# Turning and placing the rank stacks on VectorE and ScalarE instead of TensorE

## Chip, cores and metric

The kernel runs on one core of one Trainium2 chip. The metric is the device time in microseconds; each kernel is run several times and the median counts. TensorE multiplies 128x128 blocks; VectorE and ScalarE do elementwise work and may read PSUM, POOL (GpSimd) works on SBUF alone here, and the SP queue issues all DMAs.

## The reference, cut to what matters

x has 64 sequences of 64 tokens with 1024 features. Four residual layers are applied in a row, each with its own per-sequence choice:

```
x = x + (x W0^T + 2 * sum over experts of gate * (x A0^T) B0^T)   # top 2 of 8 experts, language bias on the gate
x = x + W1[condition]^T x                                         # 64x64 mixing of the 64 tokens of a sequence
x = x + (x B2[a]^T) A2[a]^T                                       # rank 16, adapter a of 64
x = x + (x W3^T + b3 + 2 * (x A3[m]) B3[m])                       # rank 16, adapter m of 32
```

The kernel multiplies the dense layers together beforehand (W0 and W3 with their identities, and the small matrices of the adapters through them), so that one pass over x is left, plus the products of low rank. For the two adapters it has to form the hidden values h2 and h3 (16 per sequence), and multiply them with rows of the combined adapter matrices.

## The kernel before, in words

**Tiling.** A tile is 128 tokens, that is two sequences of 64 (BT = 2, TB = 64); there are 32 tiles, handled in 16 pairs (a, b). Every fp32 operand of a product is split into a rounded high part and a low rest, and three matmuls (high-high, high-low, low-high) make one product. Half of the work is cut by one level of Winograd's form of Strassen's method, which takes four sums of blocks of x (S1 to S4) per pair. They are made by POOL (sums, L715), rounded by ScalarE (s_hi) and their rests taken by VectorE (s_lo).

**Stages.** Up to about 346 us the weights are combined (groups of matmuls, L1407). After that the pairs run: step(j) for j = 0 to 14 and last(15). Each engine has its own program, written out by hand in order, with semaphores between them: fore(j) (TensorE L1522, ScalarE L964, VectorE L1314), then the rest of step(j) (L1585, L986, L1339) or last(j) (L1622, L1007, L1360). POOL's order is in L739 and L755. In numbers(j), a and b are the tiles of pair j, a1 and b1 those of the pair before, and b2 = 2j-3 is the odd tile of the pair before those two, whose last product is finished at the start of pair j. back is set from the second pair on, fin from the third on (14 pairs).

**The ranks.** For a tile, the mixed products (L1458) leave the hidden values of both adapters in the first 64 columns of an output bank. For h2:
- ScalarE rounds them to the high part (h2_hi, L892), two instructions of 64 partitions, one per sequence, into h2stack, a 128x128 tile with the axes sequence, rank, copy, high or low. A sequence fills only its own 64 columns; the rest was zeroed once by POOL (L645, L646).
- VectorE writes the low part (h2_lo L1219, stack_lo L1212), again two instructions.
- TensorE transposes the stack to PSUM (h2_rows, L1484), ScalarE copies it to SBUF as h2T (h2T_copy, L907).
- TensorE multiplies h2T with the adapter rows up2 (ranks2, L1499), which adds h2's part to the output and yields h3's hidden values (semaphore pe_h3).

h3 goes the same way over h3_hi (L899), h3_lo (L1225), h3_rows (L1489), h3T_copy (L911) and ranks3 (L1509). Then add_bias (L1262) adds the bias to the three pieces of the bank and writes the output tile outb, and only after that (semaphores dve_out) may the next tile's mixed products use the bank.

**Order around the change.** At the start of a pair VectorE does h3_lo(b2), Ra_raw, Lb_lo, Ra_lo of the pair before, add_bias(b2), x1_lo, h2_lo(a1), the hidden sums and the gates. TensorE does the plain product of tile a with the transpose of h3(b2) after three of its eight blocks and ranks3(b2) after five, the hidden product, then mixed(a1), which waits for Ra_lo and all three pieces of add_bias(b2). POOL starts its sums after place_udb(a1) (L708), which waits for the last ranks2 (pe_up2). In the calm middle of the pair come h2(a1), h3(a1) and h2(b1). The last pair has the same parts in an order of its own.

Of the kernel before, what the change touches and what calls it, by code (L numbers as in the profile page):

```python
# [16 lines left out]
def build(nc, x, stat, mov, a0, wr, wc, u3, u2k, d3k, bias3, lang_ids, ids, out):  # L17
# [137 lines left out]
    with ctx:  # L155
# [116 lines left out]
        h2stack = sb("h2stack", [P, BT, RANK, 2, 2], F32R)  # L272
        h3stack = sb("h3stack", [P, BT, RANK, 2, 2], F32R)
# [26 lines left out]
        ps_hgT, ps_h2T, ps_h3T = ps_s[:, 0:TOKENS], ps_s[:, TOKENS:2 * TOKENS], ps_s[:, 2 * TOKENS:3 * TOKENS]  # L300
# [10 lines left out]
        def plain_bank(t):  # L311

            return ps_d[0] if (t // 2 + t) % 2 == 0 else ps_d[2]

# [5 lines left out]
        def sem(name):  # L320
# [21 lines left out]
        act_h2, act_h2T, act_h3, act_h3T, act_hgT = map(sem, ("act_h2", "act_h2T", "act_h3", "act_h3T", "act_hgT"))  # L342
# [7 lines left out]
        dve_h2, dve_h3, dve_hgT = map(sem, ("dve_h2", "dve_h3", "dve_hgT"))  # L350
# [6 lines left out]
        pe_group, pe_hl, pe_ud, pe_rep, pe_h, pe_mix, pe_h2T, pe_h3, pe_up2, pe_hgT, pe_h3T = map(  # L357
            sem, ("pe_group", "pe_hl", "pe_ud", "pe_rep", "pe_h", "pe_mix", "pe_h2T", "pe_h3", "pe_up2", "pe_hgT", "pe_h3T"))
# [3 lines left out]
        CONSTS = 6  # L362
        SETS = BT + 8
# [14 lines left out]
        def _(sp):  # L378
# [189 lines left out]
            sp.wait_ge(pool_const, CONSTS)  # L568
# [68 lines left out]
        def _(pool):  # L637
# [7 lines left out]
            nc.gpsimd.memset(h2stack[:, :, :, :, :].rearrange("p b r h e -> p (b r h e)").bitcast(F32), 0.0).then_inc(pool_const, 1)  # L645
            nc.gpsimd.memset(h3stack[:, :, :, :, :].rearrange("p b r h e -> p (b r h e)").bitcast(F32), 0.0).then_inc(pool_const, 1)  # L646
# [124 lines left out]
        def _(act):  # L771
# [120 lines left out]
            def h2_hi(t):  # L892
                act.wait_ge(pe_h, t + 1)
                for b in range(BT):
                    rows = slice(b * TB, (b + 1) * TB)
                    last = round_to(h2stack[rows, b, :, :, 0], hidden(t, rows, slice(b * RANK, (b + 1) * RANK)))
                last.then_inc(act_h2, 1)

            def h3_hi(t):  # L899
                act.wait_ge(pe_h3, t + 1)  # L900
                for b in range(BT):
                    rows = slice(b * TB, (b + 1) * TB)
                    last = nc.scalar.activation(h3stack[rows, b, :, :, 0], hidden(t, rows, slice(BR + b * RANK, BR + (b + 1) * RANK)),
                                                ACT.Copy, scale=SCALE3)
# [59 lines left out]
            def fore(j, back, fin):  # L964
                a, b, a1, b1, b2 = numbers(j)
                if fin:
                    h3_hi(b2)
                if back:
                    Ra_hi(j - 1)
                if fin:  # L970
                    h3T_copy(b2)
# [3 lines left out]
                if back:  # L975
                    h2_hi(a1)
                gate_exp(a)
                ud_hi(b)
                after_P1(j)
                if back:  # L980
                    h2T_copy(a1)
# [4 lines left out]
            def step(j, back, fin):  # L986
# [10 lines left out]
                if back:  # L997
                    h2_hi(b1)
                ud_hi(a + 2)
# [3 lines left out]
                if back:  # L1003
                    h2T_copy(b1)
# [35 lines left out]
        def _(dve):  # L1040
# [88 lines left out]
            nc.vector.tensor_scalar(rbias[:, :, :], rbias[:, :, :], LANG_BIAS, None, ALU.mult).then_inc(dve_set, 1)  # L1129

# [8 lines left out]
            dve.wait_ge(dve_set, BT + 7)  # L1139
# [72 lines left out]
            def stack_lo(t, rows, b, cols, stacked, scale):  # L1212

                src = out_bank(t, 0)[rows, cols][:, :, None].to_broadcast([TB, RANK, 2])
                return nc.vector.scalar_tensor_tensor(out=stacked[rows, b, :, :, 1], in0=src, scalar=scale,
                                                      in1=stacked[rows, b, :, :, 0].bitcast(F32), op0=ALU.mult,
                                                      op1=ALU.subtract)

            def h2_lo(t):  # L1219
                dve.wait_ge(act_h2, t + 1)  # L1220
                for b in range(BT):
                    last = stack_lo(t, slice(b * TB, (b + 1) * TB), b, slice(b * RANK, (b + 1) * RANK), h2stack, 1.0)
                last.then_inc(dve_h2, 1)

            def h3_lo(t):  # L1225
                dve.wait_ge(act_h3, t + 1)
                for b in range(BT):
                    last = stack_lo(t, slice(b * TB, (b + 1) * TB), b, slice(BR + b * RANK, BR + (b + 1) * RANK), h3stack, SCALE3)
                last.then_inc(dve_h3, 1)

# [167 lines left out]
        def _(pe):  # L1398
# [85 lines left out]
            def h2_rows(t):  # L1484
                pe.wait_ge(dve_h2, t + 1)
                nc.tensor.transpose(ps_h2T, h2stack[:, :, :, :, :].rearrange("p b r h e -> p (b r h e)").bitcast(F32),
                                    ident[:, :]).then_inc(pe_h2T, 1)

            def h3_rows(t):  # L1489
                pe.wait_ge(dve_h3, t + 1)  # L1490
                nc.tensor.transpose(ps_h3T, h3stack[:, :, :, :, :].rearrange("p b r h e -> p (b r h e)").bitcast(F32),
                                    ident[:, :]).then_inc(pe_h3T, 1)

# [5 lines left out]
            def ranks2(t):  # L1499
                pe.wait_ge(act_h2T, t + 1)  # L1500
# [8 lines left out]
            def ranks3(t):  # L1509
                pe.wait_ge(act_h3T, t + 1)  # L1510
# [11 lines left out]
            def fore(j, back, fin):  # L1522
# [9 lines left out]
                plain(a, range(0, 3))  # L1532
                if fin:
                    h3_rows(b2)
# [226 lines left out]
```

## Time and profile before

| | |
|---|---|
| median of 3 runs | 904.51 us (903.81 to 905.5) |
| the profiled execution | 906.27 us |
| span of its profile | 904.5 us |
| TensorE busy, granted clock | 895.8 us (99%), 1.00 |
| VectorE busy | 557.5 us (62%) |
| ScalarE busy | 345.8 us (38%) |
| POOL busy | 234.9 us (26%) |

Times in the profile count from the start of the span, in microseconds. The profiled execution is one run, 1.8 us of which lie outside the span. L12 is line 12 of the kernel above. A row that names one engine's instruction may end with the idle time before it and who ended it.

### The profile page before, as it was taken

The page shows a single profiled execution, that of the slowest core. Times are in us where ns is not written, and L with a number is a line of the kernel's source. Part 1 is how long each engine was busy: PE and PEld are TensorE (multiplying, and loading weights), DVE is VectorE, ACT ScalarE, POOL GpSimd, SP SyncE. Part 2 cuts the span into 40 slices and gives each one's busy share as a digit, 9 for nine tenths or more (in the row PEclk, how much of TensorE's full clock was granted, in tenths as well). Part 3 has the DMA queues.
Part 4 walks back from the last instruction along what each step waited for, and adds up shares of the span by engine and source line. Part 5 has one row for each costly group of instructions (what it writes and reads, how often), then busy time and mean ns, then how long its engine had stood idle before and what let it go on. Part 6 is the DMA issues. An engine that isn't in the chain of part 4 may idle for free.

```text
span 904.5 us, 14862 instructions
## 1 busy us (share of the span) xinstructions
PE 895.8 (99%) x4758; PEld 795.4 (88%) x4758; DVE 557.5 (62%) x1421; ACT 345.8 (38%) x800; POOL 234.9 (26%) x379
## 2 busy tenths in 40 slices
PE   9999999999999999999999999999999999999997
PEld 7888888888888888998998998998998999989997
DVE  6655444354357526567667677677676676676675
ACT  5543343333334333333434433434424334334333
POOL 1000010011010003523424433424415325324240
PEclk9999999999999999999999999999999999999999
DMA  7978686999663564666766766766666567666664
GB/s 248 309 252 287 208 252 202 311 338 270 186 190 119 172 211 132 189 179 185 218 181 189 216 188 182 210 194 192 190 197 213 168 189 226 182 174 216 184 199 155
DMA packets 105602, 187.69 MB, mean 208 GB/s; under 512 B 15926, under 2 KB 66870, under 8 KB 105526
## 3 DMA queue, kind: packets, MB, share of 16 engines
q1 hardware_dynamic: 105526, 186.76, 67.7%
q8 instruction: 38, 0.62, 0.3%
q14 instruction: 38, 0.31, 0.1%
HBM read 143.20 MB, written 49.81 MB: 213 GB/s over the span
## 4 chain that ended last, share of the span: by engine, by line
PE 92%; DMA 3%; SPq 2%; issue 1%; POOL 1%; DVE 0%; ACT 0%; DVEq 0%; POOLq 0%
PE ps_o L1407 28%; PE ps_d L1433 17%; PE ps_w L1441 13%; PE ps_d L1441 10%; PE ps_s L1407 9%; PE ps_o L1454 5%; PE ps_d L1448 4%; PE ps_o L1465 2%; DMA mdraw<-t 2%; PE ps_s L1471 1%; SPq L445 1%; PE ps_w L1448 1%; DMA chunk_a_raw<-mov 1%; SPq L473 1%; PE ps_o L1503 1%
## 5 line engine op out<-in xcount | busy, mean ns | idle before, releaser
L1042 DVE TENSOR_TENSOR stat_lo<-stat_raw,stat_hi 128x1024 fp32r<-128x1024 f32 (+1 forms) x127 | 146.3, 1152 | 25.8 <-ACT stat_hi L773 23.5
L773 ACT ACTIVATE stat_hi<-stat_raw 128x1024 fp32r<-128x1024 f32 (+1 forms) x127 | 116.8, 933 | 20.5 <-POOL stat_raw L657 6.3
L1433 PE MATMUL ps_d<-w_hi,stat_hi 128*128 128x512 f32 x256 | 105.0, 410 | 0.0
L1433 PE MATMUL ps_d<-w_lo,stat_hi 128*128 128x512 f32 x256 | 101.1, 395 | 0.0
L1433 PE MATMUL ps_d<-w_hi,stat_lo 128*128 128x512 f32 x256 | 100.8, 394 | 0.0
L1407 PE MATMUL ps_o<-chunk_a_hi,stat_hi 128*128 128x512 f32 x216 | 84.4, 391 | 0.6 <-DVE chunk_a_lo L1042 0.6
L1407 PE MATMUL ps_o<-chunk_a_lo,stat_hi 128*128 128x512 f32 x216 | 84.1, 389 | 0.0
L1407 PE MATMUL ps_o<-chunk_a_hi,stat_lo 128*128 128x512 f32 x216 | 84.0, 389 | 0.0
L682 POOL CAST w_hi<-mdraw 128x512 fp32r<-128x512 f32 x32 | 19.6, 614 | 208.8 <-DMA mdraw<-t 208.8
L657 POOL TENSOR_TENSOR stat_raw<-stat_raw,ident 128x128 f32<-128x128 f32 x40 | 21.8, 546 | 186.3 <-DMA stat_raw<-stat 186.3
L1407 PE MATMUL ps_o<-chunk_b_hi,stat_hi 128*128 128x512 f32 x152 | 59.1, 389 | 0.0
L1407 PE MATMUL ps_o<-chunk_b_hi,stat_lo 128*128 128x512 f32 x152 | 59.1, 389 | 0.0
L1407 PE MATMUL ps_o<-chunk_b_lo,stat_hi 128*128 128x512 f32 x152 | 59.1, 389 | 0.0
L1433 PEld LDWEIGHTS ps_d<-w_lo,stat_hi 128*128 128x128 f32 x256 | 48.1, 188 | 11.4
L1433 PEld LDWEIGHTS ps_d<-w_hi,stat_hi 128*128 128x128 f32 x256 | 48.5, 189 | 9.8 <-DVE udb L1246 0.3
L1433 PEld LDWEIGHTS ps_d<-w_hi,stat_lo 128*128 128x128 f32 x256 | 48.4, 189 | 8.1
L1259 DVE TENSOR_TENSOR outb<-ps_o,bias_row 128x356 f32<-128x356 f32 (+1 forms) x93 | 42.0, 507 | 13.1 <-PE ps_o L1465 12.6
L1407 PEld LDWEIGHTS ps_o<-chunk_a_hi,stat_hi 128*128 128x128 f32 x216 | 40.5, 188 | 9.9 <-DVE chunk_a_lo L1042 1.3
L773 ACT ACTIVATE y_hi<-y_raw 128x356 fp32r<-128x356 f32 x48 | 24.0, 499 | 64.8 <-DVE y_raw L1288 48.8
L1407 PEld LDWEIGHTS ps_o<-chunk_a_lo,stat_hi 128*128 128x128 f32 x216 | 40.6, 188 | 8.5
L1407 PEld LDWEIGHTS ps_o<-chunk_a_hi,stat_lo 128*128 128x128 f32 x216 | 40.6, 188 | 8.2
L718 POOL TENSOR_TENSOR stat_raw<-stat_raw 128x512 f32<-128x512 f32 x32 | 45.3, 1415 | 5.5 <-DMA stat_raw<-x 4.0
(226 smaller groups left out, 2269.7 us busy)
## 6 DMA issues: line engine op xcount, KB each, us to landing
up<-tu SPq DMA_DIRECT2D x124, 256.0 KB, 4.4
stat_raw<-stat SPq DMA_DIRECT2D x59, 512.0 KB, 4.2
mdraw<-t SPq DMA_DIRECT2D x128, 208.0 KB, 2.9
stat_raw<-x SPq DMA_DIRECT2D x32, 512.0 KB, 3.5
out<-outb SPq DMA_DIRECT2D x30, 512.0 KB, 5.4
t<-md_a SPq DMA_DIRECT2D x16, 576.0 KB, 5.8
rows_raw<-x SPq DMA_DIRECT2D x32, 256.0 KB, 3.5
chunk_a_raw<-mov SPq DMA_DIRECT2D x24, 256.0 KB, 5.2
```

Of the source, the lines that this page charges most:

```text
L657: nc.gpsimd.tensor_tensor(out=raw[:, s, :], in0=raw[:, s, :], in1=ident[:, :], op=ALU.add).then_inc(pool_stat, 1)
L682: last = nc.gpsimd.tensor_copy(w[part][:, :, MD_AT:P_AT].rearrange("p k (q r) -> p k q r", r=RANK), rows.rearrange("p q (k r) -> p k q r", ...
L718: nc.gpsimd.tensor_tensor(out=dst, in0=in0, in1=in1, op=op).then_inc(pool_s, 1)
L773: return nc.scalar.activation(dst, src, ACT.Copy)
L1042: return nc.vector.tensor_tensor(out=dst, in0=src, in1=rounded.bitcast(F32), op=ALU.subtract)
L1259: nc.vector.tensor_tensor(out=dst[:, OX[n]], in0=out_bank(turn, n)[:, OK[n]], in1=bias_row[:, OX[n]], op=ALU.add).then_inc(dve_out[n], 1)
L1407: last = nc.tensor.matmul(ps_g[g % BANKS][:, :], st[g % RING][a][:, k, :], mchunk[c % 2][v][:, k, :], start=k == 0 and m == 0, stop=k == K ...
L1433: last = nc.tensor.matmul(plain_bank(t)[:, 0:WCOLS], rows[a][:, k, :], w[c][:, k, :], start=k == 0 and m == 0, stop=k == KB - 1 and m == l ...
L1441: last = nc.tensor.matmul(ps[:, 0:SH], rows[a][:, k, :], weights[c][:, k, :], start=first and k == 0 and m == 0, stop=k == HALF_KB - 1 and ...
L1448: last = nc.tensor.matmul(ps, hgT[t % 2][a][:, :], b03[c][:, cols], start=first and m == 0, stop=m == len(PASSES) - 1, skip_group_check=True)
L1454: last = nc.tensor.matmul(out_bank(turn, n)[:, 0:OW[n]], mix[turn % 2][a][:, :], y[t % 2][c][:, Y[n]], start=first and m == 0, stop=m == l ...
L1465: return nc.tensor.matmul(out_bank(turn, n)[:, OK[n]], stackT[:, :], up[:, OX[n]], start=first, stop=True, skip_group_check=True)
```

## The change

The stack tile loses its axis of sequences: h2stack and h3stack are now 128x64, each token holding only the 64 columns of its own sequence. One VectorE transpose turns the 32x32 blocks of the stack in place on the grid (tile turned, 128x64). After it each of its eight 32x32 squares has to be put to its rows and columns of h2T or h3T; VectorE copies the four of the first sequence, ScalarE the four of the second. The squares off the diagonal of sequences are zeroed once, at the start, by two VectorE copies of 128x128. POOL's two memsets, TensorE's 64 transposes and the copies out of PSUM go. ScalarE's placing now stands directly behind its stack operations (in front of Ra_hi, gate_exp, ud_hi and others), VectorE's inside h2_lo and h3_lo. ranks3(b2) moves one block of the plain product later, and in the last pair one rank product changes its place. The SP queue's first load_mix waits for VectorE's set-up (dve_set) instead of POOL's. In the diff below, the first place_squares, the h2T_copy and h3T_copy and the lines of fore with h3_hi are ScalarE's; the two tensor_copy in the set-up, turn_ranks, the second place_squares and h3_lo are VectorE's; the rest is TensorE's.

```diff
-        h2stack = sb("h2stack", [P, BT, RANK, 2, 2], F32R)
-        h3stack = sb("h3stack", [P, BT, RANK, 2, 2], F32R)
+        h2stack = sb("h2stack", [P, RANK, 2, 2], F32R)
+        h3stack = sb("h3stack", [P, RANK, 2, 2], F32R)
+        turned = sb("turned", [P, 4 * RANK])
...
+        def h2_place(turn):
+            return 2 * turn + (0 if at(turn, TURN_A) else 1)
+        def h3_place(turn):
+            return 2 * turn + (3 if at(turn, TURN_B) else 2)
+        def squares(rows, b):
+            return [(rows[b * 4 * RANK + q:b * 4 * RANK + q + SQUARE, i:i + SQUARE], turned[i:i + SQUARE, q:q + SQUARE])
+                    for i in range(b * TB, (b + 1) * TB, SQUARE) for q in range(0, 4 * RANK, SQUARE)]
...
-            sp.wait_ge(pool_const, CONSTS)
+            sp.wait_ge(dve_set, SETS)
...
+            def place_squares(rows):
+                for dst, src in squares(rows, 1):
+                    last = round_to(dst, src)
+                last.then_inc(act_turned, 1)
             def h2T_copy(t):
-                act.wait_ge(pe_h2T, t + 1)
-                round_to(h2T[:, :], ps_h2T).then_inc(act_h2T, 1)
+                act.wait_ge(dve_turned, h2_place(t))
+                if not at(t, 0):
+                    act.wait_ge(pe_up2, t)
+                    act.wait_ge(pe_h3, t)
+                place_squares(h2T)
             def h3T_copy(t):
-                act.wait_ge(pe_h3T, t + 1)
-                round_to(h3T[:, :], ps_h3T).then_inc(act_h3T, 1)
+                act.wait_ge(dve_turned, h3_place(t))
+                if not at(t, 0):
+                    act.wait_ge(pe_out[2], t)
+                place_squares(h3T)
...
                 if fin:
                     h3_hi(b2)
+                    h3T_copy(b2)
                 if back:
                     Ra_hi(j - 1)
-                if fin:
-                    h3T_copy(b2)
...
+            for rows in (h2T, h3T):
+                nc.vector.tensor_copy(rows[:, :], mixraw[:, :]).then_inc(dve_set, 1)
...
+            def turn_ranks(stacked, place):
+                if place > 1:
+                    dve.wait_ge(act_turned, place - 1)
+                    dve.wait_ge(dve_placed, place - 1)
+                nc.vector.transpose(turned[:, :], stacked[:, :, :, :].rearrange("p r h e -> p (r h e)").bitcast(F32)
+                                    ).then_inc(dve_turned, 1)
+                dve.wait_ge(dve_turned, place)
+            def place_squares(rows):
+                for dst, src in squares(rows, 0):
+                    last = nc.vector.tensor_copy(dst, src)
+                last.then_inc(dve_placed, 1)
             def h3_lo(t):
...
                 last.then_inc(dve_h3, 1)
+                dve.wait_ge(dve_h3, t + 1)
+                turn_ranks(h3stack, h3_place(t))
+                if not at(t, 0):
+                    dve.wait_ge(pe_out[2], t)
+                place_squares(h3T)
...
             def ranks3(t):
-                pe.wait_ge(act_h3T, t + 1)
+                pe.wait_ge(act_turned, h3_place(t))
+                pe.wait_ge(dve_placed, h3_place(t))
...
-                plain(a, range(0, 3))
-                if fin:
-                    h3_rows(b2)
-                plain(a, range(3, 5))
+                plain(a, range(0, 6))
                 if fin:
                     ranks3(b2)
-                plain(a, range(5, KB)).then_inc(pe_hl, 1)
+                plain(a, range(6, KB)).then_inc(pe_hl, 1)
```

h2_lo gets the same lines as h3_lo with h2's semaphores (pe_up2 and pe_h3 for pe_out[2]). In step(j) ScalarE's h2T_copy moves from behind after_P1 to behind h2_hi(a1), and from behind Lb_hi to behind h2_hi(b1).

## Rows read from the trace of the kernel before

**Rows 1.** The page: busy time, share of the span, instructions of each engine.

```profile
PE 895.8 (99%) x4758; PEld 795.4 (88%) x4758; DVE 557.5 (62%) x1421; ACT 345.8 (38%) x800; POOL 234.9 (26%) x379
```

**Rows 2.** Busy time by stage: length, PE, PEld, DVE, ACT, POOL, clock, DMA.

```profile
487.00:870.00 383.00, 381.89 (x2241) 353.03 (x2240) 266.01 (x814) 148.04 (x407) 141.60 (x221) 1.00 0.65 195
```

**Rows 3.** The chain of waits, 556 to 592 us: start, length, what.

```profile
563.30 1.95 PE ps_w L1441 x12
...
585.45 1.57 PE ps_o L1454 x9
...
588.97 0.11 PE ps_s L1486
```

**Rows 4.** Groups by form: busy us and mean ns, then idle before.

```profile
L773 ACT ACTIVATE h2stack<-ps_o 64x32 fp32r<-64x32 f32 x62 | 12.0, 193 | 15.4 <-PE ps_o L1454 15.0
...
L773 ACT ACTIVATE h2T<-ps_s 128x128 fp32r<-128x128 f32 x32 | 8.8, 274 | 1.8 <-PE ps_s L1486 1.8
...
L1486 PE MATMUL ps_s<-ident,h2stack 128*128 128x128 f32 x32 | 8.7, 271 | 0.0
...
L1234 DVE COPY va<-ps_s 64x32 f32<-64x32 f32 x32 | 5.7, 178 | 2.5 <-PE ps_s L1471 2.0
```

**Rows 5.** Timeline of the start of a pair: start, length, instruction.

```profile
579.00 0.39 DVE L1215 SCALAR_TENSOR_TENSOR h3stack<-ps_o,h3stack 64x32 fp32r<-64x32 f32 x2 [0.31 <-ACT h3stack L903]
...
579.09 1.29 POOL L718 TENSOR_TENSOR stat_raw<-stat_raw 128x512 f32<-128x512 f32 x1
...
580.35 1.28 POOL L718 TENSOR_TENSOR rows_raw<-rows_raw,stat_raw 128x512 f32<-128x512 f32 x1
580.52 1.50 DVE L1042 TENSOR_TENSOR y_lo<-y_raw,y_hi 128x356 fp32r<-128x356 f32 x1
...
580.79 0.27 PE L1491 MATMUL ps_s<-ident,h3stack 128*128 128x128 f32 x1
...
580.82 0.48 PE L1433 MATMUL ps_d<-w_hi,stat_hi 128*128 128x512 f32 x1
...
581.61 1.59 POOL L718 TENSOR_TENSOR stat_raw<-stat_raw 128x512 f32<-128x512 f32 x1
...
582.70 1.35 DVE L1259 TENSOR_TENSOR outb<-ps_o,bias_row 128x312 f32<-128x312 f32 x3 [0.68 <-PE ps_o L1465]
...
583.34 1.30 POOL L718 TENSOR_TENSOR rows_raw<-rows_raw,stat_raw 128x512 f32<-128x512 f32 x1
...
585.28 0.42 PE L1454 MATMUL ps_o<-y_hi,mix_hi 128*128 128x376 f32 x1
```

**Rows 6.** Timeline of VectorE's gate beside POOL, first a calm one.

```profile
565.63 0.48 DVE L1185 TENSOR_SCALAR gsel<-iota_e,topf,gw 128x8 f32<-128x8 f32 x2
566.15 0.17 DVE L1188 TENSOR_TENSOR gates<-gsel 128x8 f32<-128x8 f32 x1
...
589.40 0.62 POOL L682 CAST w_lo<-mdraw 128x512 fp32r<-128x512 f32 x1
...
589.46 1.29 DVE L1185 TENSOR_SCALAR gsel<-iota_e,topf,gw 128x8 f32<-128x8 f32 x2
...
589.98 0.75 POOL L698 TENSOR_TENSOR u2s<-mdraw,u2s 128x256 fp32r<-128x256 f32 x1
...
590.67 0.75 POOL L698 TENSOR_TENSOR d3m<-mdraw,d3m 128x256 fp32r<-128x256 f32 x1
...
590.78 0.66 DVE L1188 TENSOR_TENSOR gates<-gsel 128x8 f32<-128x8 f32 x1
```

**Rows 7.** Instructions of the tile topf: least, median and longest ns.

```profile
L1173 DVE CAST topf<-topi x32: 169/169/405, 349.4 to 879.7; 128x2 f32<-128x2 uint32 x32
```

**Rows 8.** Timeline of VectorE behind h3_lo of an even tile.

```profile
560.07 0.68 DVE L1042 TENSOR_TENSOR stat_lo<-stat_raw,stat_hi 128x512 fp32r<-128x512 f32 x1
```

**Rows 9.** Timeline of the start: TensorE's first group on a full slot.

```profile
19.42 0.19 PEld L1407 LDWEIGHTS ps_o<-chunk_a_hi,stat_hi 128*128 128x128 f32 x1 [0.34 <-DVE stat_lo L1042]
```

**Rows 10.** Timeline of VectorE in the last pair.

```profile
884.29 0.29 DVE L1042 TENSOR_TENSOR hgTb_lo<-ps_s,hgTb_hi 128x128 fp32r<-128x128 f32 x1
...
888.59 0.53 DVE L1301 TENSOR_TENSOR y_raw<-ps_d,part 128x356 f32<-128x356 f32 x1 [0.21 <-PE ps_d L1441]
```

More of the change, by code:

```diff
@@ L361, in build @@
         pe_out = [sem(f"pe_out{n}") for n in range(3)]
-        CONSTS = 6
-        SETS = BT + 8
+        CONSTS = 4
+        SETS = BT + 10
+        SQUARE = 32
         def pairs(step):
@@ L893, in h2_hi @@
                 act.wait_ge(pe_h, t + 1)
+                if not at(t, 0):
+                    act.wait_ge(dve_turned, h2_place(t - 1))
                 for b in range(BT):
                     rows = slice(b * TB, (b + 1) * TB)
-                    last = round_to(h2stack[rows, b, :, :, 0], hidden(t, rows, slice(b * RANK, (b + 1) * RANK)))
+                    last = round_to(h2stack[rows, :, :, 0], hidden(t, rows, slice(b * RANK, (b + 1) * RANK)))
                 last.then_inc(act_h2, 1)
@@ L1210, in mix_lo, with stack_lo @@
                 rest(mix[t % 2][lo][:, :], mixid[t % 2][:, :], mix[t % 2][hi][:, :]).then_inc(dve_mix, 1)
-            def stack_lo(t, rows, b, cols, stacked, scale):
+            def stack_lo(t, rows, cols, stacked, scale):
                 src = out_bank(t, 0)[rows, cols][:, :, None].to_broadcast([TB, RANK, 2])
-                return nc.vector.scalar_tensor_tensor(out=stacked[rows, b, :, :, 1], in0=src, scalar=scale,
-                                                      in1=stacked[rows, b, :, :, 0].bitcast(F32), op0=ALU.mult,
+                return nc.vector.scalar_tensor_tensor(out=stacked[rows, :, :, 1], in0=src, scalar=scale,
+                                                      in1=stacked[rows, :, :, 0].bitcast(F32), op0=ALU.mult,
                                                       op1=ALU.subtract)
+            def turn_ranks(stacked, place):
[9 more added lines that the diff above has]
+                last.then_inc(dve_placed, 1)
             def h2_lo(t):
@@ L1221, in h2_lo @@
                 for b in range(BT):
-                    last = stack_lo(t, slice(b * TB, (b + 1) * TB), b, slice(b * RANK, (b + 1) * RANK), h2stack, 1.0)
+                    last = stack_lo(t, slice(b * TB, (b + 1) * TB), slice(b * RANK, (b + 1) * RANK), h2stack, 1.0)
                 last.then_inc(dve_h2, 1)
+                dve.wait_ge(dve_h2, t + 1)
+                turn_ranks(h2stack, h2_place(t))
+                if not at(t, 0):
+                    dve.wait_ge(pe_up2, t)
+                    dve.wait_ge(pe_h3, t)
+                place_squares(h2T)
             def h3_lo(t):
@@ L1227, in h3_lo @@
                 for b in range(BT):
-                    last = stack_lo(t, slice(b * TB, (b + 1) * TB), b, slice(BR + b * RANK, BR + (b + 1) * RANK), h3stack, SCALE3)
+                    last = stack_lo(t, slice(b * TB, (b + 1) * TB), slice(BR + b * RANK, BR + (b + 1) * RANK), h3stack, SCALE3)
                 last.then_inc(dve_h3, 1)
+                dve.wait_ge(dve_h3, t + 1)
+                turn_ranks(h3stack, h3_place(t))
+                if not at(t, 0):
+                    dve.wait_ge(pe_out[2], t)
+                place_squares(h3T)
             def hidden_sum(t):
@@ L1565, in fore @@
                     pe.wait_ge(dve_Ra_raw, j)
-                plain(b, range(0, HALF_KB))
-                pe.wait_ge(dve_udb, a + 1)
-                if back:
-                    h3_rows(a1)
-                plain(b, range(HALF_KB, KB)).then_inc(pe_hl, 1)
+                plain(b, range(KB)).then_inc(pe_hl, 1)
                 if back:
                     ranks3(a1)
+                pe.wait_ge(dve_udb, a + 1)
                 gated_rows(a)
@@ L1688, in last @@
                 mixed_piece(TURN_A, a, 2, False)
-                pe.wait_ge(act_h3T, TURN_B + 1)
+                pe.wait_ge(act_turned, h3_place(TURN_B))
+                pe.wait_ge(dve_placed, h3_place(TURN_B))
                 pe.wait_ge(ld_up3_b, 16 * BT)
+                ranks(h3T, up3_b, TURN_B, 1)
                 for n in (0, 2):
                     ranks(h3T, up3_b, TURN_B, n).then_inc(pe_out[n], 1)
-                ranks(h3T, up3_b, TURN_B, 1)
-                h3_rows(TURN_A)
                 pe.wait_ge(dve_Lb, j + 1)
                 mixed_piece(TURN_B, b, 1, False).then_inc(pe_out[1], 1)
-                pe.wait_ge(act_h3T, TURN_A + 1)
+                pe.wait_ge(act_turned, h3_place(TURN_A))
+                pe.wait_ge(dve_placed, h3_place(TURN_A))
                 pe.wait_ge(ld_up3, 16 * BT * (TILES - 1))
```

52 lines of the change are left out of this document (17 added, 35 removed).

## The prediction

> **What bounds the kernel now.** I read the page first, then the busy times by stage, the chain of waits through a pair of tiles, the groups by form, and the timelines of the places that the change touches. TensorE is busy for 99% of the span [rows 1]. From 487 to 870 us, the steady part of the tile stage, it misses 1.1 of 383 us at a clock of 1.00 [rows 2]; these are 11 pairs of tiles, 34.8 us each, of 16 in all. The chain of waits through a pair is TensorE alone: 39 pieces, of which [rows 3] show three (a Winograd product, the mixed products, a transpose). So what leaves TensorE's queue is won in full, as long as nothing that TensorE waits for comes later than it gets there. The second thing to read is therefore slack, and it is small at one place, the start of a pair.
>
> **What goes: 64 TensorE transposes.** Two a tile over 32 tiles. Their own duration is 271 ns [rows 4], but they overlap their neighbours: the matmul after the one at 580.79 starts 0.03 us later [rows 5]. The chain gives each 0.11 us [rows 3]. So 64 x 0.11 = 7.0 us. Bounds: 0.10 to 0.12, 6.4 to 7.7 us. The Trainium skill (TensorE: Matmul & The Clock Gate, Part 4) has a transpose at about 275 ns in a kernel's context, which the duration matches; taken as the price it would make 17.6 us of this. The chain's own step decides for 0.11.
>
> **What VectorE gets.** Per rank product one transpose of 128x64, two waits on itself and four copies of 32x32. No row shows that transpose or that copy. Nearest for the transpose: a copy of 64x32 from PSUM in 178 ns [rows 4] below, the 0.39 us of two stack operations above [rows 5]; I take 0.2. For a copy, a cast of 128x2 takes 169 ns [rows 7], and two stack operations stand 0.2 apart; a next one may overlap, so 0.15 each, 0.6 for four. The waits I put at 0.03 each, an estimate from a gsel that ends at 566.11 and its gates at 566.15 [rows 6]. Sum 0.85 us (0.6 to 1.2), over 64 places 54 us on an engine that is busy 557.5 of 904.5 us [rows 1]: it doesn't become the bound, and costs only where something waits behind it.
>
> **What ScalarE gets.** Four copies for one of 274 ns; a 64x32 operation takes 193 ns [rows 4], so four take 0.75, 0.5 more per place, 31 us over 346 busy. It now also stands still for VectorE's transpose right behind its own stack operations. At two of the four places of a pair it stood idle there anyway. I cost it at nothing outside the last pair.
>
> **Start.** Two copies of 128x128 are put before VectorE's first full stat_lo, and TensorE waits 0.34 us for exactly that one [rows 9]. Two copies at 0.2 (bounds 0.2 to 0.6 together): +0.4 us, once. The two memsets that POOL loses and the moved wait of the SP queue lie before anything that needs them: nothing.
>
> **The calm places.** In three of a pair's four places the 0.85 us fall into slack: POOL is idle there, and what stands behind on VectorE is wanted by TensorE more than 2 us later. The tightest is h3 of the even tile: behind it stands the stat_lo that ends at 560.75 [rows 8], wanted by the Winograd product that the chain has from 563.30 [rows 3]. If that cover were gone each place would cost up to 0.85 us, 14 or 15 times.
>
> **The place that is not calm: h3 of the odd tile at the start of the next pair.** The timeline shows it [rows 5], and it looks the same in every pair. VectorE's h3 stack operations start at 579.00, and at 579.09 POOL starts its four sums, released by the same rank product; they run to 584.64. Now look at VectorE's y_lo at 580.52: two SBUF inputs, 1.50 us where this form takes 0.53, and it ends 0.4 us after POOL's second sum does. It was locked out until POOL's instruction was over. That it also hits one-input operations is in [rows 6, 7]: two gsel operations (one SBUF input) take 0.48 us when POOL is idle and 1.29 beside POOL's casts, the cast topf takes 169 ns but up to 405. And it strikes anew each time: gsel, gsel and gates end just after w_lo, u2s and d3m do, one POOL instruction each. Operations with an input in PSUM are untouched (the three outb of 582.70: 0.45 each beside POOL's sum 4).
> The new copies are SBUF to SBUF. VectorE's transpose ends near 579.65, the copies follow. First copy: waits for sum 1, to 580.4. Second: waits for sum 2, to 581.8. Third: sum 3, to 583.2. Between sums 3 and 4 POOL leaves 0.14 us; if the fourth copy slips in there, the place is done at T = 583.4, otherwise behind sum 4 at T = 584.75. Behind it in VectorE's queue stand Ra_raw, Lb_lo, Ra_lo and add_bias. From the start of Ra_raw to the end of add_bias uncontended is 0.45 + 0.45 + 0.55 + 1.35, about 2.9 us with a wait for ScalarE (0.45 to 0.55 for each operation on 356 columns, 1.35 for the three outb, [rows 5]). With T = 583.4, Ra_lo also meets sum 4 and ends at 585.05, add_bias at 586.35. TensorE asks for all three results (dve_out) before the mixed products, at 585.28 now [rows 5], 585.17 then. So it stands 1.2 us; with T = 584.75 the bias ends at 587.75, 2.6 us. The rank products of h3 (before 582.70, now one block of the plain product later) stand first; their wait is a part of the same 1.2 or 2.6. Threshold: any T beyond 582.1 costs. The place comes 14 times (pairs 2 to 15). I take T = 583.4, since the copies are short and the gap is in all pairs: 14 x 1.2 = +16.8 us; bounds 0 and 14 x 2.6 = 36.4, and 3 to 6 more where ScalarE, late with Ra_hi and its s_hi, makes h2 meet POOL's casts.
> The Trainium skill (SBUF — State Buffer, "A bandwidth-pool intuition that's wrong") says that copies and casts can take a pair of ports that VectorE shares with GpSimd, that the pair is locked for a whole instruction and that the loser blocks. By that rule the copies are caught as gsel was; the rows say the same without it, and no row here shows a copy to fp32r.
>
> **The last pair.** POOL is idle, but VectorE's queue is the tight one. hgT_lo (884.29) goes behind a placement and is wanted right behind its end; Rb_part (888.59) behind another and is wanted at its end, 889.12 [rows 10]; at the end the last h3 placement goes before six bias pieces, of 0.45 each, and it also has to wait until the rank products of the tile before have read h3T. Three times 0.85 and about 0.4 for that wait and ScalarE's longer queue: +3.0 us (bounds 1 and 4).
>
> **Sum.** Against the profiled execution, 906.27 us with a span of 904.5: -7.0 + 0.4 + 3.0 + 16.8 = +13.2, so 919.5. The median of the runs, 904.51, stands 1.76 below that execution, so 917.7 us for the median.
>
> **Rivals.**
> *1. The copies don't meet POOL (faster).* They take the port once and keep it, or a copy to fp32r on 32 partitions doesn't ask for it. Then the place is done by 580.9 at the latest, the bias ends before 585.1 and TensorE waits for nothing: 904.5 - 7.0 + 0.4 + 3.0 = 900.9; with a cheaper end 899. For: none of the stretched rows is a copy of this form, and the lock needs POOL to be in time again after each copy. Against: the cast and both gsel, three lockouts in a row.
> *2. Every copy is caught (much slower).* If the transpose is caught too, or sum 4 gets in front of the last copy: T = 584.75, 14 x 2.6, 937; with the follow-on stalls 942. For: in [rows 6] no two VectorE operations ran between two POOL instructions. Against: sum 4 waits for sum 3's semaphore, u2s and d3m have no such gap.
> *3. It cancels.* One or two copies are caught and each pair stands 0.3 us: near 905.
> *4. The transposes' time doesn't come off in full*, as they may be covered by weight loads: 0.05 each in place of 0.11 adds 3.5 us to any case. Counted inside the cases.
>
> **How the numbers follow.** A difference under 0.2% (1.8 us) is about what a measurement of this kernel can't tell from none. Contended with T near 583.4: 0.40. Every copy caught: 0.25. Slower together with the slow part of rival 3: 0.67. Rival 1: 0.27. Rival 3 within 0.2%: 0.06; the skill's price for a transpose has at most 0.02, inside faster. The likeliest case has its own range of 911 to 924. Range for 8 in 10: from 900, which takes in most of rival 1, to 938, which takes in most of rival 2. Both signs hold weight, hence the width.
>
> **What would show it.** Right: VectorE's copies to h3T at the start of a pair with gaps or durations of 0.6 to 1.3 us beside POOL's rows_raw and stat_raw sums, 0.1 to 0.2 elsewhere; TensorE's first mixed product released by VectorE's outb, its rank products by the copies; a pair of about 35.5 or more. Wrong: those copies at 0.1 to 0.2 us in a row, a pair at 34.3 and no wait of TensorE on VectorE outside the last pair. A clock below 1.00 after the new gaps would add to any of it. The start is right if TensorE's wait near 19.4 grows to 0.7; the end if the last bias piece starts some 2 us later against the last mixed product.

## The result and the profile after

The changed kernel takes 922.4 us (median of 6 runs, 921.6 to 924.1) against 905.0 us for the kernel before on the same chip (903.8 to 906.5): 1.0195 times as long, 95% interval 1.0181 to 1.0209, so slower beyond the noise, by just under 2%. Forecast were 917.7 us (900 to 938) with slower at 0.67. The profiled execution has a span of 922.3 us, against 904.5.

The page of the changed kernel, busy times, the chain by engine and by line, and one group of instructions:

```profile
PE 903.2 (98%) x4694; PEld 789.6 (86%) x4694; DVE 634.9 (69%) x1743; ACT 386.2 (42%) x992; POOL 234.4 (25%) x377
...
PE 82%; DVE 11%; issue 2%; ACT 1%; DMA 1%; SPq 1%; POOL 0%; DVEq 0%; ACTq 0%; POOLq 0%
PE ps_o L1462 26%; PE ps_w L1496 13%; PE ps_d L1488 11%; PE ps_d L1496 10%; PE ps_s L1462 9%; PE ps_o L1509 5%; DVE h3T L1260 5%; PE ps_d L1503 4%; DVE outb L1314 2%; PE ps_o L1520 1%; ACT y_hi L787 1%; DVE y_raw L1328 1%; PE ps_s L1526 1%;
...
L1260 DVE CAST h3T<-turned 32x32 fp32r<-32x32 f32 x128 | 59.0, 461 | 2.4
```

VectorE, of which the chain through a pair had nothing before [rows 3], now holds 11% of the whole chain, and the copies to h3T alone 5%. TensorE has 64 matmuls fewer and is still busier in sum [rows 1]: a matmul's end is modelled, so a wait between two can count as busy. From here on I go by spans, not by busy time. The stretch of [rows 2] in the changed kernel (columns as there):

```profile
487.00:870.00 383.00, 377.13 (x2134) 339.88 (x2133) 313.25 (x1013) 169.03 (x520) 132.66 (x211) 1.00 0.62 188
```

TensorE misses 5.9 us of it, after 1.1, at an unchanged clock of 1.00.

The start of a pair, as [rows 5] has it for before (timeline; weight loads, Winograd and plain matmuls left out):

```profile
584.20 0.39 DVE L1244 SCALAR_TENSOR_TENSOR h3stack<-ps_o,h3stack 64x32 fp32r<-64x32 f32 x2 [0.40 <-ACT h3stack L921]
...
584.29 1.29 POOL L732 TENSOR_TENSOR stat_raw<-stat_raw 128x512 f32<-128x512 f32 x1
584.63 0.25 DVE L1253 STREAM_TRANSPOSE turned<-h3stack 128x64 f32<-128x64 f32 x1
584.91 0.94 ACT L787 ACTIVATE h3T<-turned 32x32 fp32r<-32x32 f32 x4 [0.74 <-DVE turned L1253]
584.91 3.38 DVE L1260 CAST h3T<-turned 32x32 fp32r<-32x32 f32 x4
585.53 1.30 POOL L732 TENSOR_TENSOR rows_raw<-rows_raw,stat_raw 128x512 f32<-128x512 f32 x1
586.79 1.29 POOL L732 TENSOR_TENSOR stat_raw<-stat_raw 128x512 f32<-128x512 f32 x1
...
588.22 1.30 POOL L732 TENSOR_TENSOR rows_raw<-rows_raw,stat_raw 128x512 f32<-128x512 f32 x1
588.32 0.53 DVE L1328 TENSOR_TENSOR y_raw<-ps_d,part 128x356 f32<-128x356 f32 x1
588.39 0.71 PE L1520 MATMUL ps_o<-up,h3T 128*128 128x312 f32 x3
...
589.86 1.35 DVE L1314 TENSOR_TENSOR outb<-ps_o,bias_row 128x312 f32<-128x312 f32 x3
...
591.36 0.41 PE L1509 MATMUL ps_o<-y_hi,mix_hi 128*128 128x376 f32 x1 [0.43 <-DVE outb L1314]
```

ScalarE's four copies take 0.94 us beside POOL, VectorE's four 3.38. The chain of waits has VectorE's one by one:

```profile
584.91 0.70 DVE h3T L1260
...
585.62 1.24 DVE h3T L1260
...
586.88 1.23 DVE h3T L1260
...
588.12 0.17 DVE h3T L1260
```

The first three end at 585.61, 586.86 and 588.11, each as POOL's first, second and third sum ends (585.58, 586.83, 588.08). The fourth runs its 0.17 us between the third sum and the fourth. Alone, four copies take 0.72 us. The transpose before them is not held up even beside a sum: all 32 for h3 took 245 to 248 ns.

The start of a pair is not the only place where copies are caught. The next one, h2 of the even tile, now comes so late that it meets POOL's casts of w, in each of the 14 pairs (1.18 to 1.54 us for its four copies; timeline of the same pair):

```profile
593.47 0.61 POOL L696 CAST w_hi<-mdraw 128x512 fp32r<-128x512 f32 x1 [3.95 <-DMA mdraw<-t]
...
593.58 1.45 DVE L1260 CAST h2T<-turned 32x32 fp32r<-32x32 f32 x4
594.02 0.62 POOL L696 CAST w_lo<-mdraw 128x512 fp32r<-128x512 f32 x1
```

**Where the 17.8 us went.** I mark a pair by the start of TensorE's hidden product of tile a. From the 2nd to the 16th mark, 14 pairs, before takes 489.23 us and the changed kernel 503.26: +14.0. The last stretch, from the last hidden product to the end, takes 23.87 and 27.44: +3.6. The half pair between them adds 0.5, and everything ahead of the 14 pairs takes 0.3 less.

### The profile page after: what moved, and what is told of

Same layout as the page of the kernel before. It is cut to its first block, busy times and chain, and to the rows that moved or that the text cites. A ratio compares the mean times of both kernels' runs of the same rounds, so it can differ in the third digit from the quotient of the medians.

```text
span 922.3 us, 15510 instructions
## 1 busy us (share of the span) xinstructions
PE 903.2 (98%) x4694; PEld 789.6 (86%) x4694; DVE 634.9 (69%) x1743; ACT 386.2 (42%) x992; POOL 234.4 (25%) x377
## 4 chain that ended last, share of the span: by engine, by line
PE 82%; DVE 11%; issue 2%; ACT 1%; DMA 1%; SPq 1%; POOL 0%; DVEq 0%; ACTq 0%; POOLq 0%
PE ps_o L1462 26%; PE ps_w L1496 13%; PE ps_d L1488 11%; PE ps_d L1496 10%; PE ps_s L1462 9%; PE ps_o L1509 5%; DVE h3T L1260 5%; PE ps_d L1503 4%; DVE outb L1314 2%; PE ps_o L1520 1%; ACT y_hi L787 1%; DVE y_raw L1328 1%; PE ps_s L1526 1%; PE ps_w L1503 1%; DMA stat_raw<-stat 1%
## 5 line engine op out<-in xcount | busy, mean ns | idle before, releaser
L1069 DVE TENSOR_TENSOR stat_lo<-stat_raw,stat_hi 128x1024 fp32r<-128x1024 f32 (+1 forms) x127 | 136.3, 1074 | 26.1 <-ACT stat_hi L787 23.7
L1488 PE MATMUL ps_d<-w_hi,stat_hi 128*128 128x512 f32 x256 | 102.3, 400 | 0.0
L671 POOL TENSOR_TENSOR stat_raw<-stat_raw,ident 128x128 f32<-128x128 f32 x40 | 24.0, 600 | 184.6 <-DMA stat_raw<-stat 184.6
L1260 DVE CAST h3T<-turned 32x32 fp32r<-32x32 f32 x128 | 59.0, 461 | 2.4
L732 POOL TENSOR_TENSOR rows_raw<-rows_raw,stat_raw 128x512 f32<-128x512 f32 x32 | 42.4, 1324 | 2.3
```

Of the source, the lines that this page charges most:

```text
L671: nc.gpsimd.tensor_tensor(out=raw[:, s, :], in0=raw[:, s, :], in1=ident[:, :], op=ALU.add).then_inc(pool_stat, 1)
L732: nc.gpsimd.tensor_tensor(out=dst, in0=in0, in1=in1, op=op).then_inc(pool_s, 1)
L1069: return nc.vector.tensor_tensor(out=dst, in0=src, in1=rounded.bitcast(F32), op=ALU.subtract)
L1260: last = nc.vector.tensor_copy(dst, src)
L1488: last = nc.tensor.matmul(plain_bank(t)[:, 0:WCOLS], rows[a][:, k, :], w[c][:, k, :], start=k == 0 and m == 0, stop=k == KB - 1 and m == l ...
```

## The experiments

The table gives every run by the same marks: the ratio to the kernel before in runs on the same chip, then, from the profiled execution, the mean and the shortest of the 14 pairs, the mean time in a pair from VectorE's second h3 stack operation to TensorE's first mixed product (start to mixed), and the last stretch.

| kernel | ratio (95% interval) | mean pair | shortest | start to mixed | last stretch |
|---|---|---|---|---|---|
| before | 1 | 34.95 | 34.61 | 6.03 | 23.87 |
| changed | 1.0195 (1.0181, 1.0209) | 35.95 | 35.31 | 6.96 | 27.44 |
| e1_pool_waits | 1.0224 (1.0207, 1.0241) | 35.93 | 34.79 | 5.98 | 27.53 |
| e2_act_eight | 1.0072 (1.0052, 1.0093) | 34.78 | 34.23 | 5.96 | 27.68 |
| e3_dve_two | 1.0063 (1.0042, 1.0083) | 34.92 | 34.41 | 5.98 | 27.39 |
| e4_dve_three | 1.0175 (1.0158, 1.0192) | 35.64 | 35.20 | 6.89 | 27.42 |
| e5_idle_turns | 1.0058 (1.0045, 1.0071) | 34.89 | 34.62 | 6.02 | 27.77 |
| e6_tail | 1.0059 (1.0040, 1.0079) | 34.89 | 34.17 | 5.97 | 27.72 |
| e7_rows_first | 1.0019 (1.0004, 1.0034) | 34.65 | 34.16 | 5.95 | 27.64 |
| e8_tail_by_tensor | 0.9973 (0.9962, 0.9985) | 34.85 | 34.16 | 5.86 | 23.98 |
| e9_before_rows | 1.0000 (0.9990, 1.0009) | 34.83 | 34.60 | 6.04 | 23.76 |
| e10_sums_late | 1.0047 (1.0030, 1.0064) | 34.90 | 34.39 | 5.95 | 27.58 |

The ratios rest on several runs each, the other columns on one execution. That one is the slowest of six runs for the changed kernel (924.1 us), the fastest of four for e2 (907.8) and the slowest of twelve for e8 (906.3), so differences of 0.1 or 0.2 us in the mean pair are not read from the table. From e2 to the changed kernel the mean pairs give 16.4 us, the ratios 11.1.

My theory at this point: each VectorE copy at the start of a pair is locked out by one POOL sum (the lock theory). The rival: the copies cost by their number, in VectorE's and ScalarE's queues, whatever POOL does (the queue theory).

**e1_pool_waits** takes POOL away from the copies.

```diff
                 if back:
                     place_udb(a1)
+                if fin:
+                    pool.wait_ge(dve_placed, h3_place(b2))
                 sums(j)
```

> POOL's four sums at the start of a pair wait until VectorE has placed its four squares of the odd tile's h3. Lock theory (each copy to h3T is locked out while one POOL sum runs, three per pair): the copies take 0.17 each, start to start 0.18, 0.72 for the four in place of 3.38 us; the sums begin about 1.3 us later than in the changed kernel, which has slack behind them; TensorE's first mixed product of a pair waits for nothing or at most 0.1 us. 11 pairs come at 34.5 in place of 35.99 us each, and the time falls by 14 x 1.3 to 1.5, to 902 to 905 us. If the sums, late by 1.3 us, are themselves what ScalarE and the next stacks need, the time stops at 908 to 912. Queue theory (the copies cost by their number in VectorE's and ScalarE's queues, with or without POOL): the copies' time hardly changes and the time stays at 920 to 924, or is longer.

Measured: the copies did what the lock theory says, and the time did not. The group of VectorE's copies to h3T, by line and form, in this kernel:

```profile
L1263 DVE CAST h3T<-turned 32x32 fp32r<-32x32 f32 x128 | 21.8, 170 | 2.4
```

170 ns a copy in place of 461: 37.2 us less of VectorE. Yet 924.6 us and a mean pair of 35.93. POOL's queue and what follows it, later in the same pair (timelines of POOL, ScalarE and VectorE):

```profile
591.17 2.20 POOL L732 TENSOR_TENSOR rows_raw<-rows_raw,stat_raw 128x512 f32<-128x512 f32 x1
...
593.41 0.63 ACT L790 ACTIVATE rows_hi<-rows_raw 128x512 fp32r<-128x512 f32 x1 [1.71 <-POOL rows_raw L732]
594.06 0.40 ACT L790 ACTIVATE h2stack<-ps_o 64x32 fp32r<-64x32 f32 x2
...
595.20 1.50 DVE L1263 CAST h2T<-turned 32x32 fp32r<-32x32 f32 x4
...
595.50 0.61 POOL L696 CAST w_hi<-mdraw 128x512 fp32r<-128x512 f32 x1 [2.13 <-DMA mdraw<-t]
```

The time of 924.6 us lies above all that the lock theory had for this run, and beside the 920 to 924 of the queue theory, whose condition, copies as long as before, did not hold. The sums started 1.4 us later than in the changed kernel, and the fourth then met VectorE's stat_lo (591.00, 1.22 us): this time POOL was the one held up, 2.20 us where a sum alone takes 1.29 or 1.30. ScalarE waited for it, h2 of the even tile came late, and its copies ran into POOL's next casts. TensorE waited further on, for stat_lo and h3T of the even tile. The table's marks separate the two effects. From the stack operations to the first mixed product e1 is as fast as before (5.98 for 6.03, against 6.96), so what the lock did at the start of a pair is gone. From there to the hidden product of tile b it takes 16.4 us, where the changed kernel takes 15.4. So the copies' part of the lock theory is shown; that POOL had slack for it was wrong, or so it seemed (e10 takes it up).

**e2, e3, e4** change at the 14 busy places alone how many of the eight squares VectorE copies: none, two, three. ScalarE copies the others.

```diff
-            return [(rows[b * 4 * RANK + q:b * 4 * RANK + q + SQUARE, i:i + SQUARE], turned[i:i + SQUARE, q:q + SQUARE])
-                    for i in range(b * TB, (b + 1) * TB, SQUARE) for q in range(0, 4 * RANK, SQUARE)]
+            every = [...]
+            cut = 0 if place in BUSY_PLACES else 4
+            return every[cut:] if b else every[:cut]
+        BUSY_PLACES = [h3_place(t) for t in range(1, TILES - 4, 2)]
```

> At the 14 places of the odd tile's h3 (pairs 2 to 15) ScalarE places all eight squares and VectorE none; the other 50 places stay. Lock theory: a copy of ScalarE is not held up by POOL, 0.225 to 0.235 us each, so the place is done about 1.9 us after the turn (near 586.8 on the clock of the changed kernel, where VectorE's last copy now ends at 588.3); VectorE goes straight on to Ra_raw and has add_bias ready in time. TensorE waits at most 0.1 to 0.3 us per pair, and the time is 902 to 907 us. Rival (ScalarE standing behind the turn and doing more copies is what makes the pair longer, not VectorE's lockouts): 0.9 us more on ScalarE in every pair, and the time stays above 918. Queue theory: VectorE loses 0.7 us of four copies and ScalarE gains 0.9, and the time falls by at most 14 x 0.7, to 912.

> At the same 14 places VectorE places two squares and ScalarE six. Lock theory: VectorE's first copy waits for sum 1 and the second for sum 2, so two copies take 0.7 + 1.24 = 1.9 us and VectorE goes on 1.4 us earlier than in the changed kernel; TensorE's wait before the mixed products (0.4) and at h3's rank products (0.3) goes, and the time is 902 to 908 us. Queue theory, a cost linear in the number of VectorE's copies: half of the loss comes back, 912 to 914.

> At the same 14 places VectorE places three squares and ScalarE five. Lock theory: the third copy is held by sum 3 just as in the changed kernel, and only the fourth, which slipped into the gap before sum 4 in 0.17 us, is missing: 3.2 in place of 3.38 us. The time stays at 918 to 922, close to four copies and far from two. Queue theory: a quarter of the loss comes back, 917 to 918, and the steps from four to three and from three to two are alike.

Measured: 909.9, 909.7 and 920.4 us. Two copies took 1.96 us together at most places, three 3.2. By number of copies (0, 2, 3, 4) the ratios are 1.0072, 1.0063, 1.0175 and 1.0195: nothing for the first two, 10.1 us for the third (0.72 a pair), 1.8 us for the fourth, which the intervals hardly tell from none. A cost by number would be even; this one has its step where a copy is caught by the third sum, and so has the column from the start to the mixed product. The threshold worked out beforehand, a place done by 582.1 with VectorE's stack operations at 579.00, fits: counted from those, e3's copies end after 2.66 us (581.7 on that clock), e4's after 3.91 (582.9), the changed kernel's after 4.09 (583.1, forecast 583.4). ScalarE's own part grew as VectorE's shrank, and its six or eight copies cost the start nothing. The step holds a second lock as well: the copies to h2T meet POOL's casts in 13 of e4's 14 pairs and in none of e3's. e2 at the start of a pair (timelines of POOL, ScalarE and VectorE):

```profile
579.81 1.29 POOL L739 TENSOR_TENSOR stat_raw<-stat_raw 128x512 f32<-128x512 f32 x1
...
580.44 1.90 ACT L794 ACTIVATE h3T<-turned 32x32 fp32r<-32x32 f32 x8 [0.74 <-DVE turned L1260]
...
582.90 1.10 DVE L1076 TENSOR_TENSOR y_lo<-y_raw,y_hi 128x356 fp32r<-128x356 f32 x1 [1.50 <-ACT y_hi L794]
584.02 1.35 DVE L1322 TENSOR_TENSOR outb<-ps_o,bias_row 128x312 f32<-128x312 f32 x3
```

ScalarE's eight copies pass beside POOL's sums at 0.24 us each, and the bias is done at 585.37. But 909.9 is above the 902 to 907 expected, 909.7 above the 902 to 908 of e3, and both are above before. Three things were open: what a transpose is worth, what the calm places cost, and the last pair.

**e5_idle_turns** puts 58 transposes back into TensorE's queue of e2, unused.

```diff
+            def idle_turn():
+                nc.tensor.transpose(ps_s[:, TOKENS:2 * TOKENS], ident[:, :], ident[:, :])
```

> As e2_act_eight, and TensorE makes 58 transposes of its identity into the part of ps_s that nobody uses now, at the places of its queue where the kernel before turned the stacks (four a pair); nobody reads them. It asks what a transpose is worth on TensorE. By the chain of waits of the kernel before (0.11 us each): 58 x 0.11 = 6.4 us over e2_act_eight, 914 to 917 us, a pair 0.44 longer. By rival 4 of the prediction (0.03 to 0.05 each, covered by weight loads, as TensorE's busy time in 14 pairs, 487.0 before and 485.2 in e2_act_eight, 1.8 for 56 transposes, seems to say): 2 to 3 us, 911 to 913. By the page's 0.275: 16 us.

Measured: nothing that a run can tell, 909.8 us beside 909.9 for e2 (1.0058 beside 1.0072). All three sizes expected were wrong. But the shortest pair grew from 34.23 to 34.62, which is 0.10 a transpose, the price of the chain. The waits of TensorE's weight loads for udb, in e2 and then in e5 (us in total, times, longest):

```profile
PEld ps_s L1545 <- DVE udb L1309: 2.6, 11, 0.4
```

```profile
PEld ps_s L1545 <- DVE udb L1309: 0.6, 3, 0.2
```

So a transpose is worth 0.1 us only in a pair in which TensorE waits for nothing. In e2 a part of the time that it leaves goes into waiting for VectorE (2.0 us of these waits are gone in e5), and adding it back fills the wait. For the rest of the 56 x 0.1 us these rows do not account.

**e6_tail** is e2 with two moves in the last pair.

```diff
-                h2_lo(b1)
                 hgT_lo(b)
+                h2_lo(b1)
...
-                h3_lo(b1)
                 Rb_raw(j)
+                h3_lo(b1)
```

> As e2_act_eight, and in the last pair VectorE makes hgTb_lo before it turns and places h2 of the odd tile, and the first y_raw of S[3] (Rb_raw) before it turns and places h3. If these two placements are what TensorE waits for there (0.9 and 1.0 us in e2_act_eight), both waits go or fall under 0.2, and the end comes 1.5 to 1.9 us earlier, with nothing changed up to the last pair. Rival (the placements are then late themselves, and TensorE waits for h2T and h3T in place of the two): less than 0.5 us.

Measured: the rival. The last stretch stayed at 27.72. TensorE's waits of 0.9 for hgTb_lo and 1.0 for y_raw went, and in their place it waited 1.1 for outb and 0.9 more for h3T.

**e7_rows_first** is e6 and a swap in every pair.

```diff
-                La_raw(j)
                 hidden_rows(b)
+                La_raw(j)
```

> As e6_tail, and in each pair VectorE makes udb of the odd tile (hidden_rows) before the first y_raw of La (La_raw), 0.44 us earlier. It asks whether the placement of h3 of the even tile, called calm and costed at nothing, is what is left of the pair: in e2_act_eight a pair takes 34.74 us on average, 0.29 over before's 34.90 less four transposes of 0.11, and TensorE's gated_rows waits 0.1 to 0.2 for udb and the mixed product behind it. If so, udb comes before TensorE asks, a pair takes 34.45 to 34.55, and the time falls by 14 x 0.2 to 0.25, some 3 us, under that of the kernel before. Rival (DMA or another wait sets the pair): no change within 1 us.

Measured: 1.0019, 906.3 us (903.1 to 911.6), a mean pair of 34.65, and nine of the 14 pairs between 34.16 and 34.30, that is 34.61 less four transposes of 0.1. The wait for udb is gone from the list. From e6 to e7 the ratio falls by 0.0040, 3.6 us, though not to under before, and the mean is above the 34.45 to 34.55 expected. So VectorE's queue up to udb was too long by a little in every pair. That the placement of h3 of the even tile is what made it so is read from the traces (see the calm places below); no run took that one placement away. The longer pairs (35.35, 35.36, 37.03) I followed only in the third: there POOL's cast w_hi waited until 762.57 for its DMA, and TensorE stood 1.8 us. Before has longer pairs too (35.51, 35.65).

**e8_tail_by_tensor** is e7 up to the last pair, but in it, and for its last three tiles alone, TensorE turns the stacks as before. The 128x128 stacks lie in the w tiles, which are free by then.

```diff
+        FIRST_LAST = TILES - 3
+        h2last, h3last = [w[part][:, 0, 0:BT * 4 * RANK].rearrange("p (b r h e) -> p b r h e", b=BT, h=2, e=2) for part in (hi, lo)]
...
             def h2T_copy(t):
+                if t >= FIRST_LAST:
+                    act.wait_ge(dve_turned, h2_place(t))
+                    round_to(h2T[:, :], ps_h2T).then_inc(act_turned, 1)
+                    return
```

**e9_before_rows** is the kernel before with e7's swap alone.

> As e7_rows_first up to the last pair, but the last three tiles' stacks (six turns) are turned by TensorE and placed by one ScalarE copy of 128x128 each, in the order of the kernel before; VectorE has no transpose and no square there. In e6_tail and e7_rows_first the stretch from the last hidden product to the end stayed 27.6 to 27.7 us (27.4 in the changed kernel, 23.9 in the kernel before) although two waits of TensorE were moved away; others took their place. If VectorE's queue as a whole bounds the last pair (it is busy nearly throughout from 883 us, and six turns give it 6 x 1.05 us), the stretch falls to 24.0 to 24.5 and the time to 902 to 903.5 us, 0.997 to 0.999 of the kernel before. Rival (the last pair is longer for another reason, the smaller slack of the data or ScalarE): the stretch stays above 26.5.

> The kernel before with e7_rows_first's one swap alone (udb of the odd tile before the first y_raw of La in each pair). A control: in the kernel before TensorE's wait for udb came once, 0.2 us. If the swap only repairs what the change made late, nothing: 0.999 to 1.001 of the kernel before, a pair as before. If it is a gain by itself, so is a part of e7's and e8's: below 0.998.

Measured: e8's last stretch is 23.98 us, and the time 902.7 us (900.2 to 906.3), 0.9973 of before (0.9962 to 0.9985): a version that beats both. e9 is 1.0000 (0.9990 to 1.0009), so the swap only repairs. So the six turns and placements lengthened the last pair, and by e6 not at one place. That it is VectorE's share of them is not separated: e8 also takes ScalarE's squares away, and brings TensorE's order of the last pair back to that of the kernel before.

**e10_sums_late** is e2 with POOL's sums waiting for VectorE's turn, to see what late sums cost by themselves.

```diff
+                if fin:
+                    pool.wait_ge(dve_turned, h3_place(b2))
                 sums(j)
```

> As e2_act_eight (VectorE places nothing at the start of a pair, so no copy meets POOL), and POOL's four sums wait there until VectorE has turned the odd tile's h3 stack, some 1.1 us later than they would start. In e1_pool_waits they started about 1.85 us late, the four copies took 0.72 in place of 3.38 us, and a pair stayed at 36.0. If the sums' own lateness is what that cost (ScalarE's stat_hi and rows_hi, its copies of h3 of the even tile and VectorE's stat_lo stand behind them, TensorE waited for h3T and stat_lo there), a pair of e2_act_eight grows from 34.7 to 35.2 to 35.8 and the time to 916 to 924 us. Rival (the sums have slack of over a microsecond, and e1 is slow for VectorE's copies all the same): a pair under 34.9 and 908 to 911 us.

Measured: the rival, 909.2 us, beside 909.9 for e2. POOL in the same place (timeline):

```profile
580.50 1.29 POOL L739 TENSOR_TENSOR stat_raw<-stat_raw 128x512 f32<-128x512 f32 x1 [0.62 <-DVE turned L1263]
...
584.74 1.29 POOL L739 TENSOR_TENSOR rows_raw<-rows_raw,stat_raw 128x512 f32<-128x512 f32 x1
```

POOL lost 0.62 us, not the 1.1 expected, and the sums end at 586.03, 6.7 us after ScalarE began its part of the stack (579.31); in e1 it is 8.4 (585.00 to 593.37). The first costs nothing that a run can tell; in e1 all that the free copies gave back is lost. So the sums have slack for 0.6 us; for the 1.4 of e1 it is not shown. How much of e1's loss is the later start, how much the fourth sum's being held up, and how much VectorE's copies to h2T that then meet POOL's casts, these runs do not separate.

## Why the prediction was right, and where it was off

- **The start of a pair: right, and shown.** The prediction took one copy per sum, the fourth slipping into the gap, and the place done after three sums. That is what the chain has, one lockout each; e1 shows the copies free without POOL, e2 to e4 show the cost rising with the third caught copy. The Trainium skill (SBUF — State Buffer, "Who interferes with whom") says that copies and casts can take the pair of ports that VectorE shares with GpSimd, that the first to issue has it for the whole instruction and that the other waits; these rows agree (first copy 0.70 us up to the end of a sum, 0.17 alone), for a copy to fp32r on 32 partitions too. Rivals 1 and 2 did not happen.
- **Its size: the mis-sized term.** 14 x 1.2 = 16.8 was forecast. Measured: 503.26 less the 489.23 of before, which had 56 transposes of 0.11 (6.2) in it, is 20.2 us, or 1.44 a pair. The wait meant by the 1.2, from the stack operations to the mixed product, is 6.96 less 6.03 with its transpose out, 1.04 a pair or 14.6 us. It is shorter than 1.2 mainly because Ra_lo did not meet sum 4, as the prediction had assumed (it took 0.53 us at 589.42): the bias ends 7.01 us after the stack operations begin, not 7.35. The other 5.6 us are follow-on waits, nearly all after the hidden product of tile b; the prediction had them only in its bound of 3 to 6 us. TensorE's weight loads stood 4.2 us for vparts, 3.1 for udb, 1.7 for hgTa_lo, against 0.2, 0.2 and none before.
- **The calm places: wrong.** "POOL is idle there" holds for h2 of the even tile in the kernel before (stack operations at 586.50, POOL's next cast at 588.84), but in the changed kernel this place moves with the late start and meets POOL's casts in all 14 pairs; this was in the bound and not in the sum. And "costs nothing" failed for the place named as tightest, but not where I looked. stat_lo had its cover: TensorE never waits for it in the pairs. What the placement of h3 of the even tile used up is in VectorE's queue further down, in this row of the kernel before (timeline), between h3 and the gates:

```profile
598.56 0.29 DVE L1042 TENSOR_TENSOR hgTa_lo<-ps_s,hgTa_hi 128x128 fp32r<-128x128 f32 x1 [0.91 <-ACT hgTa_hi L773]
```

  These 0.91 us were the whole reserve between h3 and udb, and a placement takes 1.05: in each of the 14 pairs of the changed kernel 0.03 is left. e7 took the wait for udb away with one swap.
- **A placement takes 1.05 us, not 0.85.** Transpose 0.25 where 0.2 was put, four copies 0.72 where 0.6 was, two gaps. ScalarE's four take 0.94, not 0.75.
- **The transposes: 0.11 was right as a price and wrong as a gain.** e7's undisturbed pairs show it (34.61 to 34.2). e5 suggests that it is had only where nobody else is late. The Trainium skill's figure for a transpose (TensorE: Matmul & The Clock Gate, Part 4), about 275 ns, is its duration here too (270 to 272), but not what it adds to the queue: the 17.6 us that it would make of all are not borne out, 58 transposes put back in e5 cost nothing that a run can tell.
- **The last pair: +3.0 forecast, measured 3.6 more with six transposes gone**, so 4.2 of waits, just above the bound of 4. e6 shows why adding three placements up was the wrong model: move two out of the way and others are late.
- **The start: +0.4 forecast, measured none.** The weight load's wait for stat_lo grew from 0.34 to 0.60, and the first plain product still starts 0.17 us earlier (340.35 for 340.52).

So the likeliest case was the one that came, for the reason given, but a part of its closeness is luck: the start of a pair was put 2.2 us too dear, and the waits behind it, 5.6 us, at nothing. By its own working the sum was 4.6 us low (+13.2 for +17.8): the pairs 3.4, the last stretch 1.2, the half pair ahead of it 0.7 with its two transposes, and the start gives 0.7 back.

## What to carry to other kernels

Before moving work from the engine that bounds to one with spare time, look at which engine runs beside it at each place. On VectorE a small copy from SBUF to SBUF took 0.17 us alone and up to 1.24 beside POOL; on ScalarE the same copy took 0.23 either way. An engine that is 62% busy can still have a stretch with under 1 us to spare. Work that makes a queue late can also carry its next instructions into another engine's work that they had passed by before. Follow its queue from the inserted work to the first result that the bounding engine asks for, over every wait, and not only to the next one. A change can be right in the steady pairs and wrong in the last: treat the last pair as a kernel of its own.

## What the runs showed of the hardware

- The lock goes both ways: in e1 the fourth POOL sum took 2.09 to 2.20 us beside VectorE's stat_lo, where a sum alone takes 1.29 or 1.30. The kernel before has it too: one sum of four takes 1.58 to 1.63 us, in [rows 5] the third, beside VectorE's y_lo.
- A 128x64 fp32 transpose on VectorE takes 245 to 248 ns and, unlike the copies, was never stretched, also in the 14 pairs where it ran beside a sum.
- A stall can cost the clock. In e8's profile TensorE stood 2.6 us for late data, up to 385.48. Stretches of 1 us from there (span; busy time and count of TensorE, weight loads, VectorE, ScalarE, POOL; granted clock, DMA share, GB/s):

```profile
385.00:386.00 1.00, 0.53 (x2) 0.49 (x3) 0.00 (x0) 0.00 (x0) 1.00 (x2) 1.00 0.83 229
...
388.00:389.00 1.00, 1.00 (x4) 0.81 (x3) 0.89 (x6) 0.44 (x2) 0.00 (x0) 0.50 0.00 0
...
391.00:392.00 1.00, 1.00 (x6) 0.78 (x6) 1.00 (x2) 0.00 (x0) 0.00 (x0) 1.00 0.00 0
```

That pair took 38.50 us. The granted clock was 0.50, the lower of its two levels (1.2 GHz of 2.4), from 387 to 390 us, after the engine had stood, and plain matmuls then started 0.43 us apart where they start 0.23 apart otherwise. From 391 us it was 1.00 again. In e7 a wait of 1.8 us up to 764.17 cost no clock (1.00 throughout).
